# Gate and expert products of a small decoder block: three float32r products of high and low halves in place of one float32 product

## The reference

```python
x = x + xattn(layernorm(x), ctx, ctx, mask, ...)
x = x + retention(layernorm(x), Wq, Wk, Wv, Wg, Wo, gnorm_w)
x = x + ffn(layernorm(x), gate_w, gate_b, expert_w, expert_b)

def ffn(x, gate_w, gate_b, expert_w, expert_b):
    g = softmax(x @ gate_w + gate_b)
    weights = g * (g >= 0.1)
    weights = weights / where(sum(weights) == 0, 1, sum(weights))
    out = 0
    for e in range(8):
        out = out + weights[:, e:e + 1] * (x @ expert_w[e] + expert_b[e])
    return out
```

## Time and profile before

| | |
|---|---|
| three executions | 218.77, 219.24, 219.28 us (median 219.24) |
| span of the profiled execution | 217.6 us (first to last instruction) |
| TensorE busy | 206.6 us, 95% |
| VectorE busy | 138.9 us, 64% |
| ScalarE busy | 108.2 us, 50% |
| GpSimd busy | 45.0 us, 21% |
| TensorE clock granted | 0.997 in the mean |

### The profile page before, as it was taken

One profiled execution on the slowest core, in us unless ns is written; L12 is line 12 of the kernel. 1 busy time (PEld: TensorE's weight loads), 2 busy tenths in 40 slices (PEclk: granted clock), 3 DMA queues, 4 the chain that ended last, 5 costly groups with the idle time before them and its releaser, 6 DMA issues.

```text
span 217.6 us, 5773 instructions
## 1 busy us (share of the span) xinstructions
PE 206.6 (95%) x2386; PEld 125.2 (58%) x2386; DVE 138.9 (64%) x283; ACT 108.2 (50%) x231; POOL 45.0 (21%) x56
## 2 busy tenths in 40 slices
PE   8798998899999999989999999999999998999992
PEld 8366654465567666656666543645758854645341
DVE  3483579986582965888985342675643636594783
ACT  2234767587784867878889761424252231101000
POOL 8307776181270500000000010100030103010000
PEclk9999999999999999999999999999999999999998
DMA  6979774355077690650000000000000000000000
GB/s 181 288 201 293 237 211 104 89 140 140 3 185 169 178 364 4 222 171 5 5 5 3 3 0 0 3 2 0 0 0 0 3 2 0 0 24 3 29 27 29
DMA packets 15792, 18.06 MB, mean 83 GB/s; under 512 B 2640, under 2 KB 14864, under 8 KB 15760
## 3 DMA queue, kind: packets, MB, share of 16 engines
q1 hardware_dynamic: 14464, 17.28, 27.2%
q10 hardware_dynamic: 1296, 0.34, 0.8%
HBM read 9.79 MB, written 0.52 MB: 47 GB/s over the span
## 4 chain that ended last, share of the span: by engine, by line
PE 77%; DVE 7%; DMA 4%; SPq 3%; ACT 3%; issue 2%; POOL 1%; DVEq 0%; ACTq 0%
PE bank L819 11%; PE bank L914 11%; PE bank L896 11%; PE bank L1130 10%; PE bank L1002 8%; PE bank L776 4%; PE bank L762 4%; DVE cneg L1730 3%; PE bank L1110 3%; PE bank L964 3%; DMA ctxT<-in_ctxT 3%; PE bank L1071 2%; PE bank L984 2%; DMA qstack<-xbo 2%; ACT prob L1412 1%
## 5 line engine op out<-in xcount | busy, mean ns | idle before, releaser
L1730 DVE TENSOR_REDUCE cneg<-bank 128x1 f32<-128x896 f32 x64 | 67.8, 1088 | 23.9 <-PE bank L819 23.8
L1412 ACT ACTIVATE prob<-bank 128x512 f32<-128x512 f32 x112 | 64.3, 600 | 14.6 <-PE bank L896 13.3
L896 PE MATMUL bank<-qstack,kstack 100*32 100x256 bf16 x896 | 43.8, 273 | 0.9 <-ACT prob L1412 0.5
L819 PE MATMUL bank<-kstack,qstack 97*32 97x448 bf16 x512 | 36.9, 354 | 2.5 <-DVE cneg L1730 0.9
L896 PEld LDWEIGHTS bank<-qstack,kstack 100*32 100x32 bf16 x896 | 23.8, 96 | 19.4 <-ACT prob L1412 3.4
L914 PE MATMUL bank<-prob,vals 128*32 128x256 f32 x448 | 34.8, 381 | 0.0
L574 POOL TENSOR_TENSOR nw<-nw,halves 128x2 f32<-128x2 f32 (+1 forms) x10 | 8.2, 825 | 118.5 <-DVE nw L1613 92.1
L1002 PE MATMUL bank<-w_late,xnT 128*128 128x512 f32 x48 | 23.5, 605 | 0.1
L819 PEld LDWEIGHTS bank<-kstack,qstack 97*32 97x32 bf16 x512 | 12.5, 95 | 9.8 <-DVE cneg L1730 4.4
L1954 DVE SCALAR_TENSOR_TENSOR x_in<-bank,nwts,x_in 128x256 f32<-128x256 f32 x32 | 15.5, 483 | 2.0 <-PE bank L1130 0.7
L914 PEld LDWEIGHTS bank<-prob,vals 128*32 128x32 f32 x448 | 12.8, 109 | 5.8 <-issue 3.8
(11 more groups left out here) (158 smaller groups left out, 250.1 us busy)
## 6 DMA issues: line engine op xcount, KB each, us to landing
kstack<-kpart SPq DMA_DIRECT2D x21, 224.0 KB
w_late<-in_w_ret SPq DMA_DIRECT2D x1, 1536.0 KB
mask_all<-in_mask SPq DMA_DIRECT2D x2, 512.0 KB, 4.4
ctxT<-in_w_exp SPq DMA_DIRECT2D x1, 1024.0 KB
kpart<-in_w_exp SPq DMA_DIRECT2D x1, 1024.0 KB
ctxT<-in_ctxT SPq DMA_DIRECT2D x2, 448.0 KB, 5.2
ctxT<-in_ctxT SPq DMA_DIRECT2D x1, 896.0 KB, 7.0
qstack<-acc SPq DMA_DIRECT2D x12, 64.0 KB, 3.6
```

Of the source, the lines that this page charges most:

```text
L819: mm = pe.matmul(out[j4:j4 + COLS, :], qstack[0:MROW + 1, h, b, qt * P + j4:qt * P + j4 + COLS], kstack[0:MROW + 1, b, h, half_ * HC:(half ...
L896: mm = pe.matmul(out[j4:j4 + COLS, hh * NQ:(hh + 1) * NQ], kstack[0:KROWS, b, h, kt * P + j4:kt * P + j4 + COLS], qstack[0:KROWS, h, b, :] ...
L1412: act.activation(prob[:, n % PROBS, :], bank[:, c.score_bank(u, jj), :], ACT.Exp).then_inc(c["prob_ready"], 1)
L1730: dve.tensor_reduce(cneg[:, st % 2, i:i + 1], bank[:, pair:pair + 2, 0:HC], AXXY, ALU.max, negate=True).then_inc(c["max_read"], 1)
```

## The change

In the experts' layer, and there alone, each float32 product a·b becomes three float32r products that add up in the same bank: high(a)·high(b), high(a)·low(b) and low(a)·high(b). High is the value cast to float32r, low is the rest. The retention and the rest stay as they were.

The weights are split once by GpSimd (`split_late`): two small operations for the gate and, for each half of the inputs, a cast and a subtraction of 128 x 2048 elements. It starts when the loads have landed and the scores of batch 0 are done (`score_ready` 56 of 112, because `exp_high` lies where the keys of batch 0 were), and TensorE waits for it at `turn_first_half`, before the retention. For the activations ScalarE casts out of PSUM to `xn_high` in place of the copy, and VectorE then subtracts (`take_low`, new, one for each tile) to `xn_low`; only this frees the bank TB. Buffers of the retention move from the rooms of `kstack` to those of `qstack` and `prob`. The loads' semaphore is parted in three. The remaining lines join semaphores.

```diff
-        late0 = kstack[:, 0, :, :].rearrange("p h k -> p (h k)").bitcast(F32)
+        exp_high = sb_over("kstack", 4 * ret_cols, "exp_high", [P, KIN, NE, D])
+        exp_low = [sb_over(of, 0, f"exp_low_{of}", [P, NE, D]) for of in ("ctxT", "kpart")]
+        late0 = qstack[:, :, :, :].rearrange("p h b q -> p (h b q)").bitcast(F32)
+        late3 = prob[:, :, :].rearrange("p n q -> p (n q)")
...
+            def split_late():
+                pool.wait_ge(s["late_loaded"], 16 * LATE_LOADS)
+                pool.tensor_copy(gate_high[:, :, :], w_gate[:, :, :]).then_inc(s["split"], 1)
+                pool.wait_ge(s["split"], 1)
+                pool.tensor_tensor(gate_low[:, :, :], w_gate[:, :, :], gate_high[:, :, :].bitcast(F32), ALU.subtract).then_inc(s["split"], 1)
+                pool.wait_ge(s["experts_loaded"], 32)
+                for c in range(KIN):
+                    pool.tensor_copy(exp_high[:, c, :, :], w_exp[c]).then_inc(s["split"], 1)
+                    pool.wait_ge(s["split"], 3 + 2 * c)
+                    pool.tensor_tensor(exp_low[c][:, :, :], w_exp[c], exp_high[:, c, :, :].bitcast(F32), ALU.subtract).then_inc(s["split"], 1)
...
                 stream_and_bias()
+                pool.wait_ge(*only.at("score_ready", NU))
+                split_late()
                 late_roots()
...
             def turn_first_half():
-                pe.wait_ge(s["late_loaded"], 16 * 10)
+                pe.wait_ge(s["late_loaded"], 16 * LATE_LOADS)
+                pe.wait_ge(s["ret_loaded"], 16)
+                pe.wait_ge(s["split"], 2 * len(SPLITS))
...
                     for c in range(KIN):
-                        mm = pe.matmul(out[:, 0:NE], xnT[:, c, t * P:(t + 1) * P], w_gate[:, c, :], start=(c == 0), stop=(c == KIN - 1))
+                        high, low = xn_high[:, c, t * P:(t + 1) * P], xn_low[:, c, t * P:(t + 1) * P]
+                        pe.matmul(out[:, 0:NE], high, gate_high[:, c, :], start=(c == 0), stop=False)
+                        pe.matmul(out[:, 0:NE], high, gate_low[:, c, :], start=False, stop=False)
+                        mm = pe.matmul(out[:, 0:NE], low, gate_high[:, c, :], start=False, stop=(c == KIN - 1))
...
+                def split_product(out, t, c, experts):
+                    high, low = xn_high[:, c, t * P:(t + 1) * P], xn_low[:, c, t * P:(t + 1) * P]
+                    pe.matmul(out, high, exp_high[:, c, experts, :], start=(c == 0), stop=False, skip_group_check=True)
+                    pe.matmul(out, high, exp_low[c][:, experts, :], start=False, stop=False, skip_group_check=True)
+                    return pe.matmul(out, low, exp_high[:, c, experts, :], start=False, stop=(c == KIN - 1), skip_group_check=True)
...
                     for c in halves:
-                        mm = pe.matmul(bank[:, PAIR_BANKS[m % 4], :], xnT[:, c, t * P:(t + 1) * P],
-                                       w_exp[c][:, 2 * pr:2 * pr + 2, :], start=(c == 0), stop=(c == KIN - 1),
-                                       skip_group_check=True)
+                        mm = split_product(bank[:, PAIR_BANKS[m % 4], :], t, c, slice(2 * pr, 2 * pr + 2))
...
+                act.copy(xn_high[:, :, t * P:(t + 1) * P], bank[:, turn_bank(kind, t), 0:D].rearrange("p (f q) -> p f q", f=KIN)
+                         ).then_inc(s["high_taken"], 1)
...
+            def take_low(kind, t):
+                dve.wait_ge(s["high_taken"], t + 1)
+                dve.tensor_tensor(xn_low[:, :, t * P:(t + 1) * P], bank[:, turn_bank(kind, t), 0:D].rearrange("p (f q) -> p f q", f=KIN),
+                                  xn_high[:, :, t * P:(t + 1) * P].bitcast(F32), ALU.subtract).then_inc(s["turn_taken"], 1)
...
                 second_stream(0, [lambda: None, lambda: decay_weights(RH + 2), lambda: decay_weights(RH + 3)])
+                take_low("n3", 0)
+                take_low("n3", 1)
                 gate_logits(0)
...
-                add_experts(1, range(0, 4))
+                add_experts(1, range(0, 2))
+                take_low("n3", 2)
+                add_experts(1, range(2, 4))
+                take_low("n3", 3)
                 gate_logits(1)
```

More of the change, by code:

```diff
@@ L9 @@
 I32 = mybir.dt.int32
+F32R = mybir.dt.float32r
 U8 = mybir.dt.uint8
@@ L129 @@
 DVE_CHAIN = 5 * STAGES
+LATE_LOADS = 7
+SPLITS = ["gate", "exp0", "exp1"]
 PER = {"k_ready": 8, "k_hi": 4, "k_rest": 4, "k_taken": 4, "k_mid": 4, "k_cut": 4, "v_ready": NVP + 2, "v_evac": NVP + 2,
@@ L234, in build, with sb_over @@
     with ExitStack() as ctx:
+        place = {}
         def sb(name, shape, dt=F32):
+            place[name] = nc.sbuf_base
             return ctx.enter_context(nc.sbuf_tensor(name, shape, dt))
+        def sb_over(of, first, name, shape):
+            return nc.alloc_sbuf_tensor_at(name, shape, F32R, offset=place[of] + first)
         def sem(name):
@@ L1443, in take_xn @@
             def take_xn(kind, t):
-                take_turn(kind, t, xnT[:, :, t * P:(t + 1) * P], bank[:, turn_bank(kind, t), 0:D].rearrange("p (f q) -> p f q", f=KIN))
+                if kind == "n2":
+                    take_turn(kind, t, xnT[:, :, t * P:(t + 1) * P], bank[:, turn_bank(kind, t), 0:D].rearrange("p (f q) -> p f q", f=KIN))
+                    return
+                assert TURNS[len(takes)] == (kind, t)
+                act.wait_ge(s["turned"], len(takes) + 1)
+                act.copy(xn_high[:, :, t * P:(t + 1) * P], bank[:, turn_bank(kind, t), 0:D].rearrange("p (f q) -> p f q", f=KIN)
+                         ).then_inc(s["high_taken"], 1)
+                takes.append((kind, t))
             def take_at(t):
                 act.wait_ge(s["turned"], TURN_AT["at", t] + 1)
-                act.activation(xnT[:, 0, t * P:(t + 1) * P], bank[:, turn_bank("at", t), 0:P], ACT.Identity, bias=bv[:, 0:1]).then_inc(s["at_half"], 1)
+                act.activation(xnT[:, 0, t * P:(t + 1) * P], bank[:, turn_bank("at", t), 0:P], ACT.Identity, bias=bv[:, 0:1])
                 take_turn("at", t, xnT[:, 1, t * P:(t + 1) * P], bank[:, turn_bank("at", t), P:2 * P], bias=bv[:, 1:2])
```

62 lines of the change are left out of this document (33 added, 29 removed).

## The result

The changed kernel takes **227.0 us** (median of 4 runs, 226.74 to 227.28) against 219.26 us (218.77 to 219.33) of the kernel before on the same chip: a ratio of 1.035, 95% interval 1.0326 to 1.0373. It is slower by 7.7 us. The forecast was 217.2 us with a range of 216.2 to 219.6; the time lies 9.8 us above the one and 7.4 above the other.

What follows compares the result with a forecast made beforehand. In the experts' stretch TensorE leads as the bound, with VectorE close behind. Tile 2's bias earlier (-1.1) and VectorE's end without waits (-0.9) gave -2.0 us: 219.24 - 2.0 = 217.2 us, range 216.2 to 219.6.

Steps and rivals of the forecast that it cites:

- the split on GpSimd: Casts and subtractions of the experts' weights, 12.9 us from 95.3 to about 108.3, hidden with 17 us to spare.
- steps 1 to 4: The tail from the turn of tile 0 to tile 2's bias: VectorE's bias add comes 1.1 us earlier, at 203.0.
- Rival (a): VectorE's cut of maxima waits for GpSimd's last subtraction, delaying TensorE's rows 1.3 to 2.1 us: 218.9 us; chance 0.33.
- A pair of experts: TensorE's expert products: a pair becomes six instructions instead of four and falls from 1.72 to 1.28 us.
- Rival (b): Slower expert products on TensorE: chance 0.10 for two periods each, 0.05 for something between.
- Gate: TensorE's gate products: six instructions instead of four, taken as 0.50 us (between 0.33 and 0.64), +0.13 us each.
- Step 1: Tiles 0 and 1: nothing gained, 0.17 us lost; TensorE's wait near 182.67 grows from 0.31 to 1.6 us.
- Steps 2 to 4: Tile 2's turn to its bias: turned at 193.35 not 194.26, gate 3's VectorE row 0.6 us earlier, bias add 1.1 earlier.
- step 3: Second subtractions on VectorE, 0.90 us, use up its 0.72 us wait and 0.17 more; row of 199.12 comes 0.6 earlier.
- Step 5: The end: after tile 2's bias VectorE runs 9.15 us without waits; those of 0.71 and 0.20 us go, -0.9 us.

Runs made afterwards that it cites:

- the filled middle: The changed kernel plus 16 unread products of 128x128 float32 ones that TensorE runs while waiting for the seventh cut of maxima: 223.1 us.

## Why the prediction was wrong

Two terms that the sum had at nothing made the miss: the split on GpSimd, called hidden, cost 3.8 us by holding VectorE, and the granted clock, never asked about, cost some 4 to 5 us. Beside them the gain of 2.0 us was 0.8, since the bias of tile 2 (steps 1 to 4) did not come earlier. Rival (a) named the first at about half its size; nothing named the second.

The steps of the tail can be read best in the kernel with the wait on GpSimd, whose profiled run had a full clock; TensorE, then VectorE:

```profile
172.32 0.44 PE L1002 MATMUL bank<-ident,xn 128*128 128x128 f32 x2
173.84 0.41 PE L1002 MATMUL bank<-ident,xn 128*128 128x128 f32 x2 [0.41 <-DVE xn_low L1887]
...
182.58 0.65 PE L1002 MATMUL bank<-ident,vals 128*128 128x128 f32 x4 [1.30 <-DVE vals L1965]
...
193.43 0.38 PE L1002 MATMUL bank<-ident,xn 128*128 128x128 f32 x2
```

```profile
176.94 0.17 DVE L1984 TENSOR_TENSOR glog<-bank,gb_row 128x8 f32<-128x8 f32 x1 [1.54 <-PE bank L1164]
...
198.84 0.17 DVE L1984 TENSOR_TENSOR glog<-bank,gb_row 128x8 f32<-128x8 f32 x1 [1.64 <-PE bank L1164]
...
203.47 0.42 DVE L2020 TENSOR_TENSOR x_in<-mask_all,bank 128x256 f32<-128x256 f32 x1 [0.66 <-PE bank L1201]
...
208.54 4.12 DVE L2014 SCALAR_TENSOR_TENSOR x_in<-bank,nwts,x_in 128x256 f32<-128x256 f32 x8
```

From the forecast to the result, each term from a run: 217.2 forecast; **+1.2** since the tail with a full clock gained 0.8 and not 2.0 (218.4, the undisturbed runs with the wait); **+3.8** the block of VectorE (222.2, the two undisturbed runs with the filled middle); **+2.2** the fallen clock in the tail (224.4, the other two; by the profiles it is 41.74 - 40.34 = 1.4, and the filled middle's tail of 41.77 says the same, so this term is more likely 1.4 than 2.2); **+2.6** the fallen clock in the middle: 227.0.

- **A pair of experts.** Right in kind: one instruction for each product. That it takes 0.213 us no run shows: it was my estimate, and with it the 1.28 us of a pair. The runs showed starts 0.23 us apart, and 0.32 at the head of a group, so a pair takes 1.38 to 1.5 us. Rival (b), slower products, is out: a pair stays under the 1.72 us of before.
- **Gate.** Under-priced: the six instructions start 0.11 us apart (181.15 to 181.82, 0.67 us), where 0.50 was taken and 0.64 was the bound. That a weight load sets a pace of 0.107 us no run shows; it was my estimate too.
- **Step 1.** Its shape was right (TensorE's wait behind pair (0,3) became 1.3 us), its size was not: the turn of y's tile 2 comes 10.26 us after the first turn with a full clock, 9.60 before, so 0.66 was lost and not 0.17. All of it is there by the gate row of tile 1, 4.62 us after the first turn for 3.96: TensorE waits 0.41 us for xn_low, so that the second turn is 1.52 us behind the first where it was 1.00 and 1.35 was taken, both gates are longer than taken, and pair (0,0) takes 1.45.
- **Steps 2 to 4.** Tile 2 is turned 21.11 us after the first turn, against 21.19: 0.1 us gained, not 0.9; the 0.5 of step 1 and three pairs at 0.1 each are missing. The gate row of tile 3 comes at 26.52 against 26.05, so 0.5 us later where step 3 had it 0.6 earlier. Tile 2's bias is added at 31.15 against 31.03, so 0.1 us later and not 1.1 earlier. This is the term of the sum that failed: -1.1 was +0.1.
- **Step 5.** Right: VectorE's end follows the bias in 9.19 us with no wait, against 10.10: -0.9.
- **The split on GpSimd.** Its length was right (two casts of 1.9 and two subtractions of 4.5 us, 96.46 to 109.47, against 95.3 to 108.3), its next user too. The word "hidden" was wrong: I looked for who waits for GpSimd's result, and left what GpSimd keeps from others to a rival.
- **Rival (a).** It named the place, the instruction and the waiting TensorE, and was given 0.33. It was what happened; but its price, 1.3 to 2.1 us, was too small. The subtraction ended at 109.47 and not at 107.5 to 108.3, since the experts' first cast began at 96.46 and not at 95.3 as the landing of the weights suggested, and the cut of maxima came 1.1 us earlier than before (104.60 for 105.74), so TensorE stood 3.8 us. And the price left out the clock: it counted idle time at its own length.
- **The clock.** Nothing in the prediction asked what a TensorE that stands still does to the clock behind it; the earlier trace rows had it at 1.00, and it was taken for given. Step 1 even made a wait of 1.6 us out of one of 0.31 and booked it as free. It was about as large a part of the miss as the block: 4.8 us by the times (2.2 and 2.6), 4.2 by the traces (1.4 and 2.8). Why the clock falls in some runs of a kernel and not in others stays open.

## To carry to other kernels

Work put on GpSimd was not hidden here where VectorE instructions with their operands in SBUF, of 8 columns, fell into it (those with two inputs stood up to 4.50 us, a cast of one input 0.75, while the reductions out of PSUM kept their 1.09): look for the small ones on the path, and put a wait of GpSimd on the instruction it must not meet. A wait of TensorE, even one that seems free because the engine is off the path there, was followed in some traces here by a stretch at half clock (3 to 7 us), so a saving that turns into a longer wait can cost more than it gives. A product made faster is worth what the chain beside it allows: here the low halves' steps gave back 1.4 of 2.2 us, and a change of order gave the old products as much.

## What I had not expected of the hardware

- The granted clock fell behind waits of 3.79 and 0.50 us in the middle (then 0.51 over 7 us), of 1.37 and 0.50 (0.50 from 108 to 111), and of 1.32 and 0.24 in the tail (0.57 over 4 us), but not in every trace: it stayed at 1.00 behind 2.02 and 0.50 us in the middle, and of the five traces with a wait of 1.28 to 1.32 us in the tail it fell in two.
- Six products of ones into a free bank went with a mean clock of 0.991 or more in all 44 runs of the four comparisons that had them; seven of these have 0.991 or 0.992, which leaves a fall in the work possible there. With three, 6 of 12 runs were under that, and in the same order with none 2 of 8.
- A GpSimd cast with one SBUF input held a VectorE instruction of two as its subtraction did (1.86 us beside a cast of 1.92, 4.48 us beside a subtraction of 4.53), and a VectorE cast of one input was held as well (0.75, 0.48, 0.41 and 0.29 us for 0.16, each time to the end of the GpSimd cast beside it).
- A float32r product was one instruction in this kernel: those of 512 columns started 0.23 us apart, those of 8 columns 0.11 us, with weight loads of 188 and 191 ns in the median.
